# A two-layer conditional residual kernel: A's rows interleaved, P on all partitions, subject words by eights, and another order of the first four pairs

## The reference

```python
# layer 0: a weight matrix (64x64) and a bias (64) are chosen by the batch's subject, 0..7
x = x + einsum('bct,bcd->bdt', x, weights[subject]) + bias[subject][:, :, None]
# layer 1: 16 rows of the low-rank A and B are chosen by the batch's adapter, 0..7
H = einsum('btd,od->bto', x, W)                       # W is 512 x 512
xa = einsum('btd,brd->btr', x, A[adapter])            # A is 8 x 16 x 512
delta = einsum('btr,bor->bto', xa, Bm[adapter])       # Bm is 8 x 512 x 16
x = x + H + delta * scalings[adapter][:, None, None]
```

## Time and profile before

| | us |
|---|---|
| median of 3 runs | 244.95 (244.68 to 245.31) |
| profiled execution, whole | 244.87 |
| its span, first to last instruction | 243.2 |
| PE busy | 231.2 (95% of the span) |
| DVE busy | 149.7 (62%) |
| ACT busy | 108.8 (45%) |
| POOL busy | 73.2 (30%) |
| PE share of the chain that ended last | 89% |
| 16 DMA engines, mean rate | 150 GB/s |

### The profile page before, as it was taken

One profiled execution on the slowest core, in us unless ns is written; L12 is line 12 of the kernel. 1 busy time (PEld: TensorE's weight loads), 2 busy tenths in 40 slices (PEclk: granted clock), 3 DMA queues, 4 the chain that ended last, 5 costly groups with the idle time before them and its releaser, 6 DMA issues.

```text
span 243.2 us, 9842 instructions
## 1 busy us (share of the span) xinstructions
PE 231.2 (95%) x2916; PEld 189.1 (78%) x2917; DVE 149.7 (62%) x259; ACT 108.8 (45%) x189; POOL 73.2 (30%) x280
## 2 busy tenths in 40 slices
PE   1989999999999999999999999999999999999991
PEld 1767888888888888888788888888888888888760
DVE  6688866675367836675368736675368754525662
ACT  2175373563526353463525445353526434344431
POOL 3466601560046300651036400656324141000000
PEclk9999999999999999999999999999999999999998
DMA  6745564745555573645546464655547364642333
GB/s 135 265 143 152 160 187 120 213 116 171 152 152 161 140 215 87 202 121 174 159 130 184 128 196 122 189 125 162 161 143 199 94 198 116 201 130 67 84 71 88
DMA packets 23621, 36.56 MB, mean 150 GB/s; under 512 B 6066, under 2 KB 6066, under 8 KB 23602
## 3 DMA queue, kind: packets, MB, share of 16 engines
q1 hardware_dynamic: 16544, 26.36, 39.1%
q10 hardware_dynamic: 7058, 9.97, 13.9%
HBM read 19.53 MB, written 16.78 MB: 149 GB/s over the span
## 4 chain that ended last, share of the span: by engine, by line
PE 89%; DVE 5%; DMA 2%; issue 1%; ACT 1%; POOL 0%; SPq 0%; DVEq 0%; ACTq 0%; POOLq 0%
PE ps L859 69%; PE ps L828 13%; PE ps L804 3%; DMA x_ring<-in_x_dram 2%; PE ps L873 1%; PE ps L877 1%; PE ps L763 1%; DVE x_lo L527 1%; DVE m_lo L510 1%; DVE x L519 1%; PE ps L798 0%; DVEq L60 0%; SPq L237 0%; DVE b_parts L491 0%; DVE o_ring L547 0%
## 5 line engine op out<-in xcount | busy, mean ns | idle before, releaser
L859 PE MATMUL ps<-m_hi,x_hi 128*128 x248 | 99.0, 399 | 0.0
L859 PE MATMUL ps<-m_hi,x_lo 128*128 x248 | 96.8, 390 | 0.0
L859 PE MATMUL ps<-m_lo,x_hi 128*128 x248 | 96.7, 390 | 0.0
L527 DVE TENSOR_TENSOR x_lo<-x,x_hi 128x512 fp32r<-128x512 f32 x64 | 44.2, 691 | 62.2 <-ACT x_hi L645 62.0
L368 POOL COPY p_pair<-p_all 64x64 f32 x128 | 40.4, 316 | 124.9 <-DVE x L519 86.6
L645 ACT ACTIVATE x_hi<-x 128x512 fp32r<-128x512 f32 x64 | 40.4, 632 | 54.0 <-ACT o_ring L658 30.0
L658 ACT ACTIVATE o_ring<-ps 128x512 f32<-128x512 f32 x60 | 35.8, 597 | 56.0 <-PE ps L859 55.8
L859 PEld LDWEIGHTS ps<-m_hi,x_hi 128*128 128x128 f32 x248 | 46.5, 188 | 10.4
L859 PEld LDWEIGHTS ps<-m_hi,x_lo 128*128 128x128 f32 x248 | 46.6, 188 | 10.1
L859 PEld LDWEIGHTS ps<-m_lo,x_hi 128*128 128x128 f32 x248 | 46.6, 188 | 9.1
L519 DVE TENSOR_TENSOR x<-ps,bias_pair 128x512 f32<-128x512 f32 x64 | 43.7, 685 | 7.9 <-PE ps L828 7.0
(11 more groups left out here) (99 smaller groups left out, 82.7 us busy)
## 6 DMA issues: line engine op xcount, KB each, us to landing
x_ring<-in_x_dram SPq DMA_DIRECT2D x124, 128.0 KB, 2.7
out_dram<-o_ring ACTq DMA_DIRECT2D x64, 128.0 KB, 2.7
out_dram<-o_ring SPq DMA_DIRECT2D x64, 128.0 KB, 2.3
a_f<-in_L_cond_A_dram SPq DMA_DIRECT2D x8, 128.0 KB
o_ring<-in_L_cond_W_dram SPq DMA_DIRECT2D x2, 256.0 KB, 4.5
o_ring<-in_L_cond_W_dram ACTq DMA_DIRECT2D x2, 256.0 KB, 5.7
x_ring<-in_x_dram ACTq DMA_DIRECT2D x4, 128.0 KB, 3.2
b_nat<-in_L_cond_Bm_dram ACTq DMA_DIRECT2D x1, 256.0 KB, 3.8
```

The source lines that it names most:

```text
L527: nc.vector.tensor_tensor(x1_lo[:, u % HELD], x1[:, u % 2], x1_hi[:, u % HELD], ALU.subtract).then_inc(x1_lo_ready, 1)
L859: mm = nc.tensor.matmul(ps[:, 2 + u % 2, :], part, m_tile(m, k, c), start=(c == 0 and part is hi and m is m_hi), stop=(c == TC - 1 and par ...
```

## The change

It has seven parts, all in the work ahead of the loop except where said.

- A's rows by turns: row 4r + g instead of 16g + r. The DMA's source is read as [16, 4, 512] with the repeat inside instead of [4, 16, 512] with the repeat outside; `b_dup` and its transposes follow (every adapter).
- `neg` is made by VectorE from the bits of the partition number (four small operations), no longer by GpSimd (one memset, four selects).
- The zeros of `a_parts` are written by GpSimd instead of VectorE.
- `p_all` has 128 partitions; VectorE adds the identity twice, rows 64 to 127 first, so GpSimd copies each half of `p_pair` from its own partitions. The wait between the two copies goes behind both (every pair).
- Subjects and places are two plain lists; GpSimd loads eight subjects every fourth pair instead of two for each pair (every pair).
- Layer 0 of pair 3 goes to the banks and columns of pair 0, not to banks 6 and 7. TensorE waits for `x1_add` of pair 0 alone ahead of pairs 2 and 3, and `x1_add` of pair 2 waits until layer 0 of pair 3 is done.
- VectorE does `x1_split(0)` ahead of `m_split_first(1)`, `x1_add(1)` behind it, and `a_split(1)` and `b_split(1)` ahead of `x1_add(3)`. ScalarE has `a_round(1)` ahead of `x1_round(1)`, and `b_round(1)` ahead of `x1_round(2)`.

```diff
-                return j + 1
+                return max(j + 1, L0_QUAD if j > 1 else 0)
...
-        def l0_out(u):
+        def l0_out(j, u):
+            if isinstance(j, int) and j == L0_QUAD - 1:
+                u = 0
...
-                sp.dma_start(a_f[:], A[ds(k, 1)].to_broadcast([G, R, T])).then_inc(a_in, 16)
+                sp.dma_start(a_f[:], A[ds(k, 1)].rearrange("k r t -> r k t").to_broadcast([R, G, T])).then_inc(a_in, 16)
...
-            (one memset and four affine_selects of neg by GpSimd)
+            pool.wait_ge(consts, 6)
+            nc.gpsimd.memset(a_parts[GR:P, :].bitcast(F32), 0.0).then_inc(rows_zeroed, 1)
+            pool.wait_ge(rows_zeroed, 1)
...
-                s = words(pool, regs, table[0:1, ds(j * 4 + W_SUBJECT, 2)], S - 1)
+                if u % 4 == 0:
+                    pool.load(regs, subjects[0:1, ds(j * 2, 8)])
+                s = [pool.snap(r, min_val=0, max_val=S - 1) for r in regs[2 * (u % 4):2 * (u % 4) + 2]]
...
                 place_p(1)
+                place_p(0)
                 pool.wait_ge(pair_ready, j * 4 + 1)
-                place_p(0)
...
+            bits = [did(nc.vector.tensor_scalar(bits_i[:, part:part + 1], pid_i[:], 2 - part, None, ALU.bitwise_and))
+                    for part in range(2)]
+            need(bits[1])
+            for part in range(2):
+                nc.vector.tensor_scalar(neg[:, part:part + 1], bits_i[:, part:part + 1], -0.5 - 0.5 * part, None,
+                                        ALU.mult).then_inc(zeroed, 1)
...
-            nc.vector.memset(a_parts[GR:P, :].bitcast(F32), 0.0).then_inc(zeroed, 1)
...
-            nc.vector.tensor_tensor(p_all[:], p_all[:], ident[0:C, 0:C].unsqueeze(1).to_broadcast([C, S, C]),
-                                    ALU.add).then_inc(p_ready, 1)
+            for side in (1, 0):
+                nc.vector.tensor_tensor(p_all[C * side:C * side + C], p_all[0:C],
+                                        ident[0:C, 0:C].unsqueeze(1).to_broadcast([C, S, C]),
+                                        ALU.add).then_inc(p_ready, 1)
...
-            x1_add(1, 1)
             x1_split(0, 0)
             m_split_first(1)
+            x1_add(1, 1)
             m_split_first(2)
             m_split_first(3)
             x1_split(1, 1)
             x1_add(2, 2)
+            a_split(1)
+            b_split(1)
             x1_add(3, 3)
             x1_split(2, 2)
-            a_split(1)
             x1_split(3, 3)
-            b_split(1)
...
             m_round_first(1)
-            x1_round(1, 1)
             m_round_first(2)
             m_round_first(3)
+            b = words(act, regs[:2], batch[0:1, 4 * XR - 2:4 * XR], B - 1)
+            a_round(1)
+            x1_round(1, 1)
             act.wait_ge(l0_done, XR)
-            load_x(act, XR - 1, words(act, regs[:2], batch[0:1, 4 * XR - 2:4 * XR], B - 1), x_in)
+            load_x(act, XR - 1, b, x_in)
+            b_round(1)
             x1_round(2, 2)
-            a_round(1)
             x1_round(3, 3)
-            b_round(1)
...
-                at_least(pe, x1_ready, j - 1)
+                at_least(pe, x1_ready, min(j - 1, 1))
```

More of the change, by code:

```diff
@@ L50, in cond_residual_layers @@
     HELD = 4
-    W_SUBJECT, W_PLACE = 0, 2
     HEAD = 4
@@ L73, in cond_residual_layers @@
         b_nat = sb("b_nat", [P, K, TC * R])
-        b_dup = sb("b_dup", [P, TC, P // R, R])
+        b_dup = sb("b_dup", [P, TC, P // G, G])
         o_ring = sb("o_ring", [P, OR, T])
         w_nat = o_ring
-        p_all = sb("p_all", [C, S, C])
+        p_all = sb("p_all", [P, S, C])
         bias_all = sb("bias_all", [P, S, C])
@@ L110, in cond_residual_layers @@
         batch = sb("batch", [1, B], I32)
-        table = sb("table", [1, PAIRS * 4], I32)
+        places = sb("places", [1, B], I32)
+        subjects = sb("subjects", [1, B], I32)
         order = sb("order", [1, K], I32)
@@ L154, in cond_residual_layers @@
         zeroed = sem("zeroed")
+        rows_zeroed = sem("rows_zeroed")
         p_ready = sem("p_ready")
@@ L320, in _ @@
                                     pattern=[[-1, P]], channel_multiplier=1).then_inc(consts, 1)
[L322 to L334, removed]
+            pool.wait_ge(consts, 6)
+            nc.gpsimd.memset(a_parts[GR:P, :].bitcast(F32), 0.0).then_inc(rows_zeroed, 1)
+            pool.wait_ge(rows_zeroed, 1)
             pool.wait_ge(bnat_in, 16)
-            regs = [pool.alloc_register(f"pool_word{i}") for i in range(2)]
+            regs = [pool.alloc_register(f"pool_word{i}") for i in range(8)]
+            order_reg = [pool.alloc_register("pool_place")]
             def dup_b(i):
-                k, = words(pool, regs[:1], order[0:1, ds(i, 1)], K - 1)
+                k, = words(pool, order_reg, order[0:1, ds(i, 1)], K - 1)
                 if isinstance(i, int) and i == 0:
@@ L361, in step @@
                 at_least(pool, x1_ready, j - (PR - 1 if n is None else min(PR - 1, HEAD - 1 + (u - HEAD) % BODY)))
-                s = words(pool, regs, table[0:1, ds(j * 4 + W_SUBJECT, 2)], S - 1)
+                if u % 4 == 0:
+                    pool.load(regs, subjects[0:1, ds(j * 2, 8)])
+                s = [pool.snap(r, min_val=0, max_val=S - 1) for r in regs[2 * (u % 4):2 * (u % 4) + 2]]
                 if n is None and j == 0:
-                    pool.wait_ge(p_ready, 1)
+                    pool.wait_ge(p_ready, 2)
                 def place_p(half):
                     rows = slice(C * half, C * half + C)
-                    nc.gpsimd.tensor_copy(p_pair[rows, slot, :], p_all[:, ds(s[half], 1), :]
+                    nc.gpsimd.tensor_copy(p_pair[rows, slot, :], p_all[rows, ds(s[half], 1), :]
                                           .rearrange("p s d -> p (s d)")).then_inc(pair_ready, 1)
@@ L729, in step @@
                     for i in range(MIXED):
-                        words(act, last_places[i], table[0:1, ds((PAIRS - MIXED + i) * 4 + W_PLACE, 2)], K - 1)
+                        words(act, last_places[i], places[0:1, ds((PAIRS - MIXED + i) * 2, 2)], K - 1)
                 if n_of_mixed(j) is None:
@@ L883, in _ @@
             pe.wait_ge(others_ready, 2)
-            first_slot, = words(pe, regs[:1], table[0:1, W_PLACE:W_PLACE + 1], K - 1)
+            first_slot, = words(pe, regs[:1], places[0:1, 0:1], K - 1)
             first_inputs(0)
@@ L902, in step @@
                 else:
-                    k = words(pe, regs[:2 if mixed else 1], table[0:1, ds(j * 4 + W_PLACE, 2 if mixed else 1)], K - 1)
+                    k = words(pe, regs[:2 if mixed else 1], places[0:1, ds(j * 2, 2 if mixed else 1)], K - 1)
                 for i in l0_pairs:
```

26 lines of the change are left out of this document (12 added, 14 removed).

## The result

The changed kernel takes 242.77 us (median of 6 runs, 242.65 to 243.01) against 245.02 us (6 runs, 244.68 to 245.31): a ratio of 0.9907, with an interval of 0.9886 to 0.9927. That is 2.25 us less, where 1.6 were forecast, inside the range. The profiled execution took 242.84 us, with a span of 241.1.

A forecast was written before the change was run, and what follows sets the result against it. TensorE, busy from 23.93 to 230.47 us, bounds the kernel, so an earlier start counts fully: 0.6 (idle at 12.2) + 0.4 (pair 3, x1_split(0)) + 0.6 (B's split) = 1.6 us off 244.87, 243.3; range 242.5 to 244.3.

The forecast's parts named there:

- The bound: From 23.93 to 230.47 us TensorE is busy for 206.53 of 206.54 us; the start's gain reaches the end unchanged.
- Zeros: Start: zeroing leaves VectorE (0.52 us), four small operations enter; one-hot matrix 0.24 us sooner, adapter order unchanged.
- g: Gain of layer 0 of pair 0: 0.6 us, bound by the transposes ending at 12.2; bounds 0.24 and 1.2.
- A's rows: A's transfer spreads over sixteen engines, 1.1 us to 0.36; a_round(0) at 10.4 to 10.7, x load landing at 11.6.
- a rival with a gain of 1.2 in all if A stays late: Front: no spread or a slow x load; g = 0.24, time 243.6; chance 0.13.
- The stage: Pair 0 to quad: 0.4 us from pair 3 and x1_split(0), 0.6 from B's split; quad at 22.3 against 23.93.
- a sequencer that had not run ahead: Before the quad: TensorE's sequencer stood at the wait for B's split, so the quad began 0.75 us behind the products.
- GpSimd: Steps of about 1.0 us a pair instead of 1.4 to 1.6; pair 7 by 21; worth nothing in steady state.
- the second rival: Second part becomes another wait (quad's x, GpSimd's pair 7 or VectorE): 0.65 us lost likely, 244.0; chance 0.13.
- Behind 230 us: What happens behind 230.47 us is touched by nothing in the change.
- The rival on TensorE's level: 12.2 to 15.7 us: matmuls at TensorE's lower level cost 3.2 us more, 246.5; chance 0.04.
- Its point of decision: The level rival decides if TensorE's level rises behind 14 us, with 1.6 us of that work caught.

The follow-up runs named there:

- a_back: Changed kernel with A's rows in the old order and A's transfer in the old shape: 244.08 us, ratio 0.9963 to the kernel before.
- stage_back: Changed kernel with old banks for pair 3 and old VectorE and ScalarE order, new front kept: 243.61 us, ratio 0.9929 to before.
- pad_vector: Changed kernel with one more VectorE instruction, a memset of one column that nothing reads: 243.04 us, ratio 0.9928 to before.
- m2_first: Changed kernel with x1_add(1) behind m_split_first(2) instead of ahead of it: 243.25 us, ratio 0.9908 to before.
- pool_back: Changed kernel with GpSimd's old step, two subject words per pair and the wait between the two p_pair copies: 244.75 us, ratio 0.9986.
- best: Changed kernel with x1_add(1) behind m_split_first(2), and VectorE instead of ScalarE copying adapter order and scalings: 243.24 us, ratio 0.9929.
- banks_back: Changed kernel with pair 3 in its old banks and behind x1_add of pair 1, new order kept: 244.20 us, ratio 0.9946.

## Why the prediction was right, and where it wasn't

**The bound.** TensorE is busy for 40.00 of 40.00 us in the stretches of the loop of the changed kernel too, and what the start gained reached the end. Right.

**Zeros.** I took 0.24 for the one-hot matrix; it moved from 3.38 to 2.94, 0.44. The memset's 0.52 went with the gap ahead of it, and the four small operations, at 2.05 to 2.46, put the casts behind them off by only 0.18 to 0.33 (2.20 to 2.38, 2.48 to 2.81). The adapter order stayed (5.42 to 5.45), as forecast.

**g.** Forecast 0.6, with the transposes as the bound; measured 12.79 - 12.03 = 0.76. They ended at 12.0 and not at 12.2, since TensorE's level rose during the last of them. The x load landed at 11.05, not 11.6.

**A's rows.** `a_round(0)` at 10.14, forecast 10.4 to 10.7. The share rose from 0.33 to 0.59 and 0.81, where I had said near 1. The term of what A is worth was wrong: the sum had 0.36 for A (0.6 less 0.24) and a rival with a gain of 1.2 in all if A stays late. a_back shows 1.38 at the quad and a gain of 1.1 in time (245.2 - 244.08), so the rival's time was about right, its inner working not.

**The stage.** Forecast for layer 1 of pair 0: 15.7, found 15.34. The wait came at the third chunk (0.48), not the fourth (0.2). The layer 1 of pair 0 ended at 18.71, forecast 18.6. Products at 21.75 without a wait; x for the quad in time. The quad at 22.30, forecast 22.3. What I had read as a sequencer that had not run ahead is the word load: in the kernel before it begins at 23.5, behind the products' wait, and the quad follows at 23.93. That the forecast met the quad so closely is in part luck: the wait at the third chunk was 0.3 longer than computed and g 0.16 larger, and TensorE's level alone moved pair 0 to 11.71 and 11.74 in stage_back and pad_vector.

**GpSimd.** This is the step that failed, though the forecast held. I wrote that its shorter steps "are worth nothing" in steady state and only that it "has pair 7 by 21" in the start, and gave it no price; the second rival named pair 7 beside other waits, also without one. It was ready at 21.24, so the number was right. But with the quad moved to 22.3 the old 22.83 was already behind it, and in the new order later still. I had compared each producer with the place of the quad before, not after. Undone, it costs 2.0 us. The sum came out right since this part of the change was there too, which is luck as far as my working goes.

**Behind 230 us** I had said that nothing changes. 0.35 us of the spans did, and it is no effect of the parts that I had priced.

**The rival on TensorE's level** is real in kind: m2_first's execution had layer 0 of pair 0 at the lower level, for 0.44 us more. Its point of decision, a rise behind 14 us, was reached in none of the fourteen profiled executions. In pool_back's the level fell again behind the quad and cost 1.6 us, a case that the prediction did not have.

## What to carry to other kernels

When a stage is moved forward by t, list every producer that it waits for, and compare each with the new time: here GpSimd's pair 7 (22.83 against a new 22.3) would have taken much of the gain, and quickening it alone gave nothing. A broadcast DMA whose outermost dimension is 4 can hold up the loads queued behind it by more than its own length; put the repeat inside. And undoing parts one by one overstates them when they need each other: the single costs here add up to far more than the 2.25 us.

## What the runs showed of the hardware

In executions that began the same work at 7.1 to 7.6 us, like instructions of TensorE became some 1.4 to 1.6 times as quick at very different times, while the granted clock read 1.00 in these stretches at either level. I read that as its rise from the lower to the higher of its two levels (1.2 and 2.4 GHz), which only the durations show. The bf16 product between the transposes takes 0.31 us at the one level and 0.22 at the other. In the changed kernel only the last is quick; in best the second already is:

```profile
11.17 0.31 PE L790 MATMUL ps<-ident_b 128*128 128x128 bf16 x1
...
11.88 0.22 PE L790 MATMUL ps<-ident_b 128*128 128x128 bf16 x1
```

```profile
9.52 0.31 PE L790 MATMUL ps<-ident_b 128*128 128x128 bf16 x1
...
10.03 0.22 PE L790 MATMUL ps<-ident_b 128*128 128x128 bf16 x1
```

In m2_first it rose inside layer 0 of pair 0, behind 12.4. Between the earliest and the latest lies about 1.4 us at the start of layer 0 of pair 0 (10.96 to 12.33), of which 0.3 is the start of the transposes (7.12 against 7.45). Where the transposes are the bound, as in the changed kernel, this is scatter that no edit here controls.

The level can also fall again, and then the granted clock does show it. In pool_back it read 0.50 from 25.75 to 29.0, behind 1.93 us in which TensorE stood still up to 24.77. In banks_back TensorE stood still for 1.71 us up to 16.57, and its clock stayed at 1.00 with the 32 matmuls of pair 3 at 0.69 us as ever.

The third thing is that a single instruction of no use on VectorE lengthened the last 25.5 us of the kernel by 0.23 us (25.74 against 25.51), 210 us later.
